# A routed-experts kernel's last stage: three tiles' routed rows weighted in place by ScalarE and added by GpSimd instead of VectorE and TensorE

## The reference

```python
logits = xf @ router_w.T + router_b
top_vals, top_idx = jax.lax.top_k(logits, K)          # K = 4 of E = 32
rw = jax.nn.softmax(top_vals, axis=-1) * SCALE
combine = jnp.einsum('tke,tk->te', jax.nn.one_hot(top_idx, E, dtype=xf.dtype), rw)
g = jax.nn.silu(jnp.einsum('th,eih->tei', xf, gate_w))
u = jnp.einsum('th,eih->tei', xf, up_w)
routed = jnp.einsum('tei,ehi,te->th', g * u, down_w, combine)
sg = jax.nn.silu(xf @ shared_gate_w.T)
su = xf @ shared_up_w.T
shared = sg * su @ shared_down_w.T
x = x + attn + routed + shared
```

## Time and profile before

| | us |
|---|---|
| median of 3 runs | 202.89 |
| lowest, highest | 202.6, 203.03 |
| span of the profiled execution | 233.7 |
| TensorE busy in it | 206.8 |
| VectorE busy | 118.0 |
| GpSimd busy | 112.4 |
| ScalarE busy | 97.0 |

### The profile page before, as it was taken

How to read it: one execution, slowest core, us unless ns; L and a number is a source line. 1 busy time by engine, 2 the same in 40 slices (tenths; PEclk the granted TensorE clock), 3 DMA queues, 4 the chain that set the end, 5 groups by cost and what they waited for, 6 DMA issues and landing times.

```text
span 233.7 us, 4585 instructions
## 1 busy us (share of the span) xinstructions
PE 206.8 (89%) x1592; PEld 150.7 (64%) x1592; DVE 118.0 (50%) x359; ACT 97.0 (42%) x242; POOL 112.4 (48%) x156
## 2 busy tenths in 40 slices
PE   8999999999889799969997598929885799999995
PEld 3677667667576498839776276616655377567764
DVE  4676898998875386313342222302051223332895
ACT  2335474478943146032481337223551473105310
POOL 3150376088847757735657263754556133451000
PEclk9999999999999899985999679997999589999999
DMA  5966999930004999954422232222213023314983
GB/s 160 385 259 243 405 438 393 452 168 3 0 4 117 394 309 399 384 198 145 146 69 89 67 108 66 75 96 84 91 45 101 15 77 114 138 67 147 368 318 112
DMA packets 14855, 42.36 MB, mean 181 GB/s; under 512 B 2661, under 2 KB 6122, under 8 KB 14064
## 3 DMA queue, kind: packets, MB, share of 16 engines
q1 hardware_dynamic: 10944, 33.03, 38.1%
q0 software_dynamic: 3456, 8.92, 11.4%
q10 hardware_dynamic: 432, 0.12, 0.2%
HBM read 34.71 MB, written 7.86 MB: 182 GB/s over the span
## 4 chain that ended last, share of the span: by engine, by line
PE 65%; DVE 9%; issue 8%; another core or an unknown queue 6%; ACT 6%; DMA 4%; POOL 2%; ACTq 0%; DVEq 0%; POOLq 0%
PE bank L1564 16%; PE bank L1577 6%; PE bank L1770 5%; PE bank L1581 4%; PE bank L1434 4%; PE bank L1444 4%; PE bank L1542 3%; DMA y_rows<-y_mem,codes 3%; PE bank L1530 3%; PE bank L1601 3%; PE bank L1504 2%; PE bank L1798 2%; DVE w_mem L1100 2%; PE bank L1459 2%
## 5 line engine op out<-in xcount | busy, mean ns | idle before, releaser
L835 POOL DMA_INDIRECT y_rows<-y_mem,codes x36 | 36.2, 1007 | 48.9 <-DVE y_mem L1163 39.1
L1564 PE MATMUL bank<-xb_mem,w_mem 128*128 128x128 f32 x384 | 51.9, 289 | 3.4 <-DVE h_mem L1157 2.1
L1564 PEld LDWEIGHTS bank<-xb_mem,w_mem 128*128 128x128 f32 x384 | 48.9, 204 | 5.4 <-issue 5.3
L827 POOL DMA_INDIRECT xg_mem<-xn_rows,codes x36 | 35.4, 983 | 12.9 <-issue 10.2
L1155 DVE TENSOR_TENSOR h_mem<-h_mem,bank 128x128 f32<-128x128 f32 x32 | 9.2, 287 | 62.7 <-ACT h_mem L638 46.8
L637 ACT ACTIVATE h_mem<-bank 128x128 f32<-128x128 f32 x32 | 8.9, 278 | 40.7 <-PE bank L1564 20.7
L1163 DVE COPY y_mem<-bank 128x256 f32<-128x256 f32 x36 | 14.3, 422 | 18.3 <-PE bank L1581 14.4
L1100 DVE TENSOR_TENSOR w_mem<-bank,w_mem 128x512 f32<-128x512 f32 x32 | 20.1, 683 | 2.8 <-PE bank L1459 2.8
L1577 PE MATMUL bank<-w_mem,h_mem 128*128 128x256 f32 x60 | 19.0, 445 | 0.5 <-DVE y_mem L1163 0.5
L627 ACT COPY xb_mem<-bank 128x512 f32<-128x512 f32 x16 | 9.3, 584 | 20.7 <-remote 10.1
L650 ACT COPY w_mem<-w_mem 128x1024 f32 x16 | 16.0, 1044 | 3.5 <-PE bank L1619 2.0
(11 more groups left out here) (167 smaller groups left out, 333.7 us busy)
## 6 DMA issues: line engine op xcount, KB each, us to landing
w_mem<-w_exp_dram SPq DMA_DIRECT2D x3, 3456.0 KB, 21.9
w_mem<-w_late_dram SPq DMA_DIRECT2D x7, 1152.0 KB, 6.8
w_mem<-y_rows SPq DMA_DIRECT2D x8, 512.0 KB, 6.8
w_mem<-w_qkvg_dram SPq DMA_DIRECT2D x2, 512.0 KB, 5.8
w_mem<-decay_dram SPq DMA_DIRECT2D x1, 1024.0 KB, 7.8
xn_rows<-w_mem SPq DMA_DIRECT2D x2, 512.0 KB, 3.2
xnt_rows<-w_mem SPq DMA_DIRECT2D x1, 1024.0 KB, 4.9
w_mem<-w_ovf_dram SPq DMA_DIRECT2D x16, 64.0 KB
```

What stands on the lines that cost most here:

```text
L827: nc.gpsimd.indirect_dma_start(xg[:, k % RING, :], None, xn_rows, bass.IndirectOffsetOnAxis(ap=codes[:, c, 0:1], axis=0),).then_inc(tok_in ...
L835: nc.gpsimd.indirect_dma_start(y_rows, bass.IndirectOffsetOnAxis(ap=codes[:, c, 1:2], axis=0), ysb[:, k % YRING, :], None, bounds_check=RO ...
L1564: last = nc.tensor.matmul(ps_gu[j][:, m * P:(m + 1) * P], w[:, o:o + P], xbT[:, p % 2, (2 * g + j) * P:(2 * g + j + 1) * P], start=(g == 0 ...
```

## The change

Tiles 0, 1 and 5 become POOL_TILES. For each of them ScalarE waits for back_in[n] and multiplies the four rows by their weights, in place (scale_rows: activation with Copy and a scale per partition), raising scaled_sb by one each. GpSimd adds the four rows to x_sb[n] one after another (add_tile: tensor_tensor add, each waiting for the last), after the tile's add_sums. ScalarE makes all diagonals behind shared_gate(0), and scales tiles 0, 1 and 5 behind shared_gate(1), (2) and (3). PE_TILES becomes (6, 7), and DVE_ROWS all rows of tiles 2, 3 and 4 and k = 0, 1 of tile 6: 14 rows on VectorE, 12 on GpSimd, 6 on TensorE. VectorE's hand-written order changes: tile 2's rows follow the sums of tiles 2 and 3, the sum of tile 5 stands after row (4, 1), and the last two sums are those of tiles 6 and 7. The stores keep their order; tile 5's now waits for tot_sb[5], from GpSimd.

```diff
--- before.py
+++ after.py
@@ -55,8 +55,9 @@
 HOT_PARTS = 2
 
 
-DVE_ROWS = {n: (0, 1, 2, 3) for n in range(5)} | {5: (2, 3)}
-PE_TILES = (5, 6, 7)
+DVE_ROWS = {n: (0, 1, 2, 3) for n in (2, 3, 4)} | {6: (0, 1)}
+POOL_TILES = (0, 1, 5)
+PE_TILES = (6, 7)
 PE_ROWS = tuple((n, k) for n in PE_TILES for k in range(TOPK) if k not in DVE_ROWS.get(n, ()))
 WARM_UP = 17
 CT = 32
@@ -415,6 +416,7 @@
         l_turn = sem("l_turn")
         back_in = [sem(f"back_in{i}") for i in range(NT)]
         diag_sb = sem("diag_sb")
+        scaled_sb = sem("scaled_sb")
         tot_sb = [sem(f"tot_sb{i}") for i in range(NT - len(PE_TILES))]
 
         block = ctx.enter_context(nc.Block())
@@ -763,11 +765,22 @@
                         a = n * TOPK + k
                         nc.scalar.activation(diag[:, i, :], ident, ACT.Copy, scale=rw[:, a:a + 1]).then_inc(diag_sb, 1)
 
+            def scale_rows(n):
+
+                act.wait_ge(back_in[n], 16)
+                for k in range(TOPK):
+                    a = n * TOPK + k
+                    nc.scalar.activation(back[:, n, k, :], back[:, n, k, :], ACT.Copy, scale=rw[:, a:a + 1]
+                                         ).then_inc(scaled_sb, 1)
+
             act.wait_ge(dn_ps, 2 * PAIRS)
             for i in range(GROUPS):
                 shared_gate(i)
-                if i < len(PE_TILES):
-                    diagonals(PE_TILES[i])
+                if i == 0:
+                    for n in PE_TILES:
+                        diagonals(n)
+                else:
+                    scale_rows(POOL_TILES[i - 1])
 
         @block.gpsimd
         def _(pool):
@@ -910,6 +923,20 @@
             for w in range(YRING):
                 pool.wait_ge(sent[w], 16 * SENT[w])
             later_rounds(pool, later)
+
+            def add_tile(i, n):
+
+                pool.wait_ge(sadd_sb, n + 1)
+                for k in range(TOPK):
+                    pool.wait_ge(scaled_sb, TOPK * i + k + 1)
+                    ins = nc.gpsimd.tensor_tensor(x_sb[:, n, :], x_sb[:, n, :], back[:, n, k, :], ALU.add)
+                    if k < TOPK - 1:
+                        step(ins)
+                    else:
+                        ins.then_inc(tot_sb[n], 1)
+
+            for i, n in enumerate(POOL_TILES):
+                add_tile(i, n)
 
         @block.vector
         def _(dve):
@@ -1319,33 +1346,26 @@
             shared_hidden(1)
             add_sums(0)
             add_sums(1)
+            shared_hidden(2)
+            add_sums(2)
+            add_sums(3)
             for k in range(TOPK):
-                add_routed(0, k)
-            shared_hidden(2)
-            add_routed(1, 0)
-            add_sums(2)
-            add_routed(1, 1)
-            add_sums(3)
-            add_routed(1, 2)
-            add_routed(2, 0)
-            add_routed(1, 3)
-            add_routed(2, 1)
+                add_routed(2, k)
             shared_hidden(3)
             add_routed(3, 0)
-            add_routed(2, 2)
             add_routed(3, 1)
-            add_routed(2, 3)
             add_sums(4)
             add_routed(3, 2)
             add_routed(4, 0)
             add_routed(3, 3)
             add_routed(4, 1)
-            add_routed(5, 2)
+            add_sums(5)
             add_routed(4, 2)
-            add_routed(5, 3)
+            add_routed(6, 0)
             add_routed(4, 3)
-            for n in PE_TILES:
-                add_sums(n)
+            add_routed(6, 1)
+            add_sums(6)
+            add_sums(7)
 
         @block.tensor
         def _(pe):
```

## The result

The change costs 4.8 us. The kernel after takes 207.71 us (207.51 to 208.09, 4 runs) against 202.96 us before: a ratio of 1.0236, interval 1.0219 to 1.0254. The sign was forecast, the size was not: 203.9 us, and 202.8 to 204.9 as the range.

The account below looks back on a forecast made before the run. The last chain was to go from TensorE's weighing to GpSimd's four adds behind tile 5's late sum: +0.9 us for the last store, +0.1 for the queue, on 202.89, giving 203.9 us; range 202.8 to 204.9.

Parts of the forecast that it names:

- The step that failed: End of the kernel: the span ends 2.1 us after the last store is issued, as in before; 234.7 on before's clock.
- Contention: GpSimd adds and VectorE rows take turns, 0.78 us a pair; group 3's hidden product starts 0.2 us late.
- The two meetings: Two overlaps of VectorE and GpSimd in before's trace, giving 0.50 + 0.28 us for a pair of add and row.
- TensorE: Weighing at the end: ten products become six, 1.81 us less, ending at 229.5 and no longer late.
- ScalarE: Scalings 0.42 us apart and 0.50 long; tile 0's four end at 218.8, just hidden before group 2's SiLU.
- Rival (c): A scaling costs 0.60 us on ScalarE, making group 2's SiLU 0.75 us late: +1.7 us, 204.6 us; chance 0.08.
- Idle time given away: VectorE has nothing to do during tile 0's adds, so the rows given away there free time that was not short.
- (a): No contention worth the name, GpSimd and VectorE run side by side: +0.3 us, 203.2 us; chance 0.18.
- (b): GpSimd gets no turn on tile 5 until VectorE's row (6,1) is done: +1.8 us, 204.7 us; chance 0.10.
- (d): GpSimd and VectorE exclude each other for the whole recorded length, 1.12 us a pair: +3.1 us, 206.0 us; chance 0.03.
- (e): Faster: unprofiled, TensorE's weighing is longer, its granted clock at the 1.2 GHz level: -3.4 us, 199.5 us; chance 0.11.
- The sign that was named: At the end: the prediction is wrong if tile 5's last add ends before VectorE's last sum.

Follow-up runs that it names:

- e1_wait: Kernel before, with one more GpSimd instruction at its end that only waits for VectorE's last sum: 207.05 us, ratio 1.0193.
- e9_early_drain: Kernel after, with one more DRAIN on GpSimd, placed where it is idle before its adds: 205.02 us, ratio 1.0104.
- e4_bank_rows: Kernel after, with VectorE's 14 rows reading their first operand from an unused half of a bank instead of back: 206.69 us, ratio 1.0188.
- e11_drain_bank: Kernel after, with both the DRAIN ahead of GpSimd's adds and VectorE's rows reading their first operand from a bank: 203.52 us, ratio 1.0027.
- e8_pool1: Kernel after, with GpSimd keeping tile 1 alone, VectorE 19 rows, TensorE 9: six runs from 203.0 to 205.5 us, ratio 1.0062.

## Why the prediction was wrong

**The step that failed** is the one from the last store to the end of the span. The prediction took it as the 2.1 us of before; it was 5.3 (233.09 to 238.4), and these 3.2 us are most of the 3.7 by which the forecast end was missed. It asked of every engine when its work is done, and of GpSimd only when its adds are; that an engine whose program was over 13.7 us before the end has a closing instruction of its own, which moves with its last work, was not asked. The number was in the trace of before, 5959 ns. As GpSimd's last add ends at 232.21 on before's clock, the DRAIN ends at 238.15 and the span 0.25 us later. Shown by e1_wait (+4.2 us by a wait alone) and e9_early_drain (-2.7 us by moving the DRAIN, though it delays tile 0's adds by 2.1 us).

**Contention: the mechanism held, its size was a little short.** The two meetings gave turns of 0.78 us a pair; 0.86 us was measured. An add of x_sb and back takes 0.73 us alone and not the 0.64 of the earlier trace rows, which fits the difference. The row of 726 ns for the product with cst was the better one: it too reads two different tensors, while those at 0.64 read parts of one. Why that makes a difference no run here tells. This term cost 0.35 us at group 3 and as much again by the last add, near the 0.6 us between the forecast and the measured last store. Taking contention away was worth 1.0 us with the drain in place (e4_bank_rows) and 1.5 us without (from e9_early_drain to e11_drain_bank).

**TensorE: right.** Its six weighed products are over at 197.23, 230.0 on before's clock, against 229.5 predicted; they bring nothing.

**ScalarE: right.** Four scalings take 1.70 us, 0.40 us apart and 0.51 us long, where 0.42 and 0.50 were taken; group 2's SiLU starts at 186.13, 0.1 us later than in before. Rival (c) didn't occur in after, but e8_pool1 shows its neighbour: the wait for the load, not the length of a scaling, is what can hold a SiLU up.

**Idle time given away: right.** VectorE waits 2.64 us before the hidden products of group 2, where before did tile 0's rows.

**The rivals.** (a) was refuted as it stood, and priced about right: with drain and contention gone the loss is 0.6 us (203.5), where (a) said 0.3 (203.2), with adds of 0.64 us instead of 0.73. (b) didn't occur: GpSimd got its turn after every row. (d) didn't occur: 0.86 us a pair, not 1.12. (e) didn't occur: the granted clock stays at 1.00 until all work is done, and it was 1.00 in the timed runs of before.

**The sign that was named** doesn't decide anything. The prediction was to be wrong if tile 5's last add ended before VectorE's last sum. It did, 232.21 against 232.48 on before's clock; but the prediction's own times had that order too, 231.5 and 231.8. What it had right is that the last stores wait for GpSimd.

Together: 4.8 us are 2.7 for the drain, 1.5 for the contention, and 0.6 for four adds, 0.81 us apart, behind a late sum, with two stores behind them (taken away in this order).

## What to carry to other kernels

An engine that is idle at the end isn't free at the end: look up its closing DRAIN in the trace (it stands in no chain while hidden) before giving it late work, and if it issued DMAs by itself, either end its work that much earlier or drain it where it idles anyway. In this kernel GpSimd's adds cost VectorE nothing only while VectorE waited or read a bank; beside rows with two SBUF operands, a pair of one add and one row took 0.86 us and two rows on VectorE alone 0.80. And a wait for a load doesn't belong ahead of an instruction that the next stage hangs on.

## What the runs showed of the hardware that was not expected

GpSimd's closing DRAIN costs 0.08 us for each DMA that GpSimd has issued since its last DRAIN, though all have landed: 0.39 us in all with none and 0.49 with 1, 3.36 with 36 (0.31 of each over a memset), 5.96 with 72, and 0.1 us once an earlier DRAIN had paid. The time passes with no engine and no DMA busy, and a semaphore wait is enough to push it behind the end. The page's chain of waits doesn't show it; SyncE's waits and the line of the block's end do.
